# A four-layer graph network on one core: 0/1 matrices made by GpSimd in layer 0's late units, list loads placed later, and the sums of layer 2's nodes split around the edge products

## The reference, cut to what matters

```python
x = _layernorm(x + L0(x, src, dst))             # attention by edges, sums by target node
x = _layernorm(x + L1(x, edge_index))           # sum of neighbours, two-layer network
x = _layernorm(x + L2(x, edge_index))           # graph attention with self loops
x = _layernorm(x + L3(x, edge_index, edge_attr_256))
# inside L0
score = exp(clip(sum(k[src] * q[dst], axis=-1) / sqrt(32), -5, 5))
wv = segment_sum(v[src] * score, dst); z = segment_sum(score, dst)
out = wv / (z + 1e-09)
# inside L2, per head: e = leaky_relu(a_src[src] + a_dst[dst]), softmax over the edges of a
# target, out = segment_sum(h[src] * alpha, dst) + bias, then + x and a layer norm
```

## Time and profile before

| | us |
|---|---|
| median of 3 executions (4677.53 to 4684.41) | 4681.47 |
| the profiled execution, own time | 4724.27 |
| its span in the trace | 4722.6 |

### The profile page before, as it was taken

How to read it: one execution, slowest core, us unless ns; L and a number is a source line. 1 busy time by engine, 2 the same in 40 slices (tenths; PEclk the granted TensorE clock), 3 DMA queues, 4 the chain that set the end, 5 groups by cost and what they waited for, 6 DMA issues and landing times. The chain is left out here.

```text
span 4722.6 us, 90136 instructions
## 1 busy us (share of the span) xinstructions
PE 4413.9 (93%) x21114; PEld 3442.3 (73%) x21114; DVE 3984.7 (84%) x12084; ACT 2635.3 (56%) x6042; POOL 3105.5 (66%) x3736
## 2 busy tenths in 40 slices
PE   6999998769999999999987999999969999999998
PEld 4666664438888888888866777777746666688887
DVE  4677778988999999999974888988867777888887
ACT  2787886544555555555553777777741111255554
POOL 4555552227777777777746888888746666588887
PEclk8999997559999999999997999999989999999999
DMA  5977777983444444444445899999855555788885
GB/s 156 244 219 223 222 219 247 296 251 106 153 152 152 148 149 152 152 152 147 150 155 161 274 275 274 277 274 274 259 158 175 175 175 175 228 260 261 263 261 173
DMA packets 911651, 970.50 MB, mean 206 GB/s; under 512 B 104938, under 2 KB 867672, under 8 KB 911306
## 3 DMA queue, kind: packets, MB, share of 16 engines
q1 hardware_dynamic: 501268, 472.10, 34.2%
q10 hardware_dynamic: 327254, 315.21, 19.6%
q0 software_dynamic: 82784, 179.41, 13.2%
HBM read 654.95 MB, written 363.57 MB: 216 GB/s over the span
## 5 line engine op out<-in xcount | busy, mean ns | idle before, releaser
L601 POOL DMA_INDIRECT layer_xg<-in_x,edge_rows x392 | 387.2, 988 | 332.7 <-PE layer_t_ps L647 240.8
L936 POOL DMA_INDIRECT nodes_near_rows<-x_d,nodes_cur x392 | 418.1, 1067 | 238.1 <-POOL nodes_cur L931 169.8
L1669 POOL DMA_INDIRECT layer_xg<-x_d,edge_rows x392 | 377.6, 963 | 211.3 <-PE layer_x_ps L1742 139.5
L1244 POOL DMA_INDIRECT nodes_near_rows<-hh_d,source_row x392 | 396.0, 1010 | 128.2 <-issue 84.7
L1059 PE MATMUL nodes_h_ps<-w_h,nodes_x2T 128*128 128x272 f32 x1568 | 392.2, 393 | 8.1 <-ACT nodes_x2T L1136 8.1
L1817 ACT ACTIVATE layer_xT<-layer_x_ps 128x512 f32<-128x512 f32 x196 | 117.0, 597 | 495.5 <-PE layer_x_ps L1742 446.2
L680 PE MATMUL layer_agg<-layer_msg,layer_hot 128*128 128x264 f32 x784 | 313.1, 539 | 65.8 <-issue 65.8
L1069 PE MATMUL nodes_hid_ps<-nodes_zT,w_a 128*128 128x256 f32 x1568 | 372.3, 380 | 0.7 <-ACT nodes_zT L1143 0.7
L662 PE MATMUL layer_kv_ps<-w_kv,layer_xT 128*128 128x512 f32 x784 | 371.2, 596 | 0.9 <-DVE layer_made L806 0.9
L1049 PE MATMUL nodes_out_ps<-w_b,nodes_hid 128*128 128x256 f32 x1568 | 371.1, 380 | 0.6 <-ACT nodes_hid L1128 0.5
L1757 PE MATMUL layer_kv_ps<-w_kv,layer_xT 128*128 128x512 f32 x784 | 370.4, 595 | 0.0
(11 more groups left out here) (241 smaller groups left out, 12724.1 us busy)
## 6 DMA issues: line engine op xcount, KB each, us to landing
layer_msg<-msg_d SPq DMA_DIRECT2D x784, 132.0 KB, 3.3
nodes_xin<-x_d SPq DMA_DIRECT2D x392, 256.0 KB
hh_d<-nodes_hh ACTq DMA_DIRECT2D x196, 264.0 KB
x_d<-layer_y ACTq DMA_DIRECT2D x196, 256.0 KB
x_d<-nodes_x2b ACTq DMA_DIRECT2D x196, 256.0 KB
nodes_hin<-hh_d SPq DMA_DIRECT2D x196, 256.0 KB
x_d<-nodes_x ACTq DMA_DIRECT2D x196, 256.0 KB
layer_xin<-x_d SPq DMA_DIRECT2D x196, 256.0 KB
```

The lines of the kernel that those rows point to most:

```text
L601: gp.indirect_dma_start(out=xg[:, c % 8, k, :], out_offset=None, in_=x, in_offset=bass.IndirectOffsetOnAxis(ap=edge_rows[:, c, k:k + 1], a ...
L936: gp.indirect_dma_start(out=near_rows[:, r, h, :], out_offset=None, in_=x1_d, in_offset=bass.IndirectOffsetOnAxis(ap=cur[:, r, h:h + 1], a ...
L1244: gp.indirect_dma_start(out=near_rows[:, u % NR, h, :], out_offset=None, in_=hh_d, in_offset=bass.IndirectOffsetOnAxis(ap=source_row[:, 2 ...
L1669: gp.indirect_dma_start(out=xg[:, c % 8, k, :], out_offset=None, in_=x3_d, in_offset=bass.IndirectOffsetOnAxis(ap=edge_rows[:, c, k:k + 1] ...
```

## The change

1. Layer 0, units from LATE = 104 on: GpSimd makes the two 0/1 matrices behind its load of x, and counts them on a new semaphore. The mean is written back into `agg` in PSUM instead of `mean_msg` in SBUF, so that PE waits before refilling `agg` for the add of x (`filled`) and not for the multiply (`divided`). The merged moments go to `t_ps`, the PSUM tile in which chunks were turned. For all units, DVE's eps-add now stands before the inversion of the norm.
2. Layer 0: GpSimd gathers the lists before chunk 7, not before chunk 4.
3. Layer 2's nodes: PE sums tile 0 ahead of the edge products and tile 1 behind them; the transposes of the shares stand between tile 0's sums and the edge products; ACT copies `own_first` before it copies the edge products. The order inside the step is otherwise as before, and so are the instructions.
4. Layer 3: SP's loads of `e_row` for chunks 2 to 7 wait until PE has turned the chunk two before.

The core of the diff (pieces with nothing but the passing of the new argument are left out):

```diff
+        def late_moments(u):
+            return t_ps[:, u % 4 * 4:u % 4 * 4 + 4].rearrange("p (h w) -> p h w", w=2) if u >= LATE else None
...
-                    if c == 4:
+                    if c == 7:
...
                 for u in range(LATE, UNITS):
                     load_x(gp, u)
+                    gp.wait_ge(summed, u - 3)
+                    for h in range(2):
+                        last = gp.tensor_scalar(hot[:, u % 4, h, :], iota[:, :], target_rel[:, 2 * u + h:2 * u + h + 1], None, ALU.is_equal)
+                    last.then_inc(late_hot, 1)
...
-                            pe.wait_ge(hot_ready, u + 1)
-                            if u >= 2:
+                            if u < LATE:
+                                pe.wait_ge(hot_ready, u + 1)
+                            else:
+                                pe.wait_ge(late_hot, u - LATE + 1)
+                            if u >= LATE + 2:
+                                pe.wait_ge(ln["filled"], u - 1)
+                            elif u >= 2:
                                 pe.wait_ge(divided, u - 1)
...
-                            u = at(U0 + 4)
-                            if u is not None:
-                                norm_invert(ve, ln, (None, 8, u))
                             u = at(U0 + 2)
                             if u is not None:
                                 ve.wait_ge(summed, u + 1)
                                 nc.vector.tensor_scalar(den[:, u % 2, :, :], agg[u % 2][:, :, D:D + H], 1e-9, None, ALU.add)\
                                     .then_inc(eps_added, 1)
+                            u = at(U0 + 4)
+                            if u is not None:
+                                norm_invert(ve, ln, (None, 8, u))
                             u = at(U0)
-                            if u is not None:
+                            if u is not None and u < LATE:
                                 if u >= 4:
                                     ve.wait_ge(summed, u - 3)
                                 one_hot_halves(ve, (None, 8, u), 4, hot, hot_ready)
...
-                                nc.vector.tensor_tensor(by_head(mean_msg[:, u % 2, :, :]), by_head(agg[u % 2][:, :, 0:D]),
+                                to = mean_msg[:, u % 2, :, :] if u < LATE else agg[u % 2][:, :, 0:D]
+                                nc.vector.tensor_tensor(by_head(to), by_head(agg[u % 2][:, :, 0:D]),
                                                         over_head(den[:, u % 2, :, :]), ALU.mult).then_inc(divided, 1)
                         c = chunk_at(s, j)(2)
...
-                                norm_merge(ve, ln, (None, 8, u), spare_ve)
+                                if u == LATE:
+                                    ve.wait_ge(copied, EC)
+                                norm_merge(ve, ln, (None, 8, u), spare_ve, late_moments(u))
...
+                                mean = mean_msg[:, u % 2, :, :] if u < LATE else agg[u % 2][:, :, 0:D]
+                                nc.vector.tensor_tensor(ln["rows"][:, u % 4, :, :], mean, xin[:, u % 8, :, :], ALU.add)\
...
+                def half_of_sums(u, h):
+                    cols = agg[u % 4][:, h * D:(h + 1) * D]
+                    nc.tensor.matmul(cols, hot[:, u % HOT, h, :], weighted[:, u % WR, h, :], start=True, stop=False)
+                    nc.tensor.matmul(cols, ones3[:, :], bias3[:, 0:D], start=False, stop=False)
+                    return nc.tensor.matmul(cols, ident[:, :], own[:, u % WR, h, :], start=False, stop=True)
...
-                        to = agg[u % 4]
...
-                        for h in range(2):
-                            cols = to[:, h * D:(h + 1) * D]
-                            nc.tensor.matmul(cols, hot[:, u % HOT, h, :], weighted[:, u % WR, h, :], start=True, stop=False)
-                            nc.tensor.matmul(cols, ones3[:, :], bias3[:, 0:D], start=False, stop=False)
-                            last = nc.tensor.matmul(cols, ident[:, :], own[:, u % WR, h, :], start=False, stop=True)
-                        last.then_inc(filled, 1)
+                        half_of_sums(u, 0)
+                    g = at(15)
+                    if g is not None and g % GU == 0:
+                        g //= GU
+                        n = of_group(g) * H
+                        pe.wait_ge(share_ready, g + 1)
+                        if g:
+                            pe.wait_ge(weighed, GU * g)
+                            pe.wait_ge(own_done, GU * g)
+                        nc.tensor.transpose(share_ps[:, 0:n], share[0:n, 0, :], ident[0:n, 0:n])
+                        nc.tensor.transpose(own_ps[:, P:P + n], share[0:n, 1, :], ident[0:n, 0:n]).then_inc(share_turned, 1)
...
-                    g = at(15)
-                    if g is not None and g % GU == 0:
...
-                        nc.tensor.transpose(own_ps[:, P:P + n], share[0:n, 1, :], ident[0:n, 0:n]).then_inc(share_turned, 1)
+                    u = at(18)
+                    if u is not None:
+                        half_of_sums(u, 1).then_inc(filled, 1)
                     u = at(15)
...
+                        own_product(u)
...
+                    g = at(15)
+                    if g is not None and g % GU == 0:
+                        g //= GU
+                        n = of_group(g) * H
+                        act.wait_ge(share_turned, g + 1)
+                        if g >= 2:
+                            act.wait_ge(own_summed, GU * (g - 1))
+                        nc.scalar.activation(own_first[:, g % 2, 0:n], own_ps[:, P:P + n], ACT.Copy, scale=-1.0 / BIG).then_inc(first_copied, 1)
                     u, e, k = at(2), at(2 + LATER), s - 2
...
                     if had(c, 8):
                         sp.wait_ge(joined, num(c) - 7)
+                    elif had(c, 2):
+                        sp.wait_ge(turned, num(c) - 1)
                     sp.dma_start(e_row[:, ring(c, 8), :], e_rows[:, bass.ds(num(c), 1), :].rearrange("p c w -> p (c w)"))\
                       .then_inc(e_in[ring(c, 8)], 16)
```

56 lines of the change are left out of this document (22 added, 34 removed).

## The result

The changed kernel takes 4631.92 us in the median of 4 executions (4627.67 to 4633.51), the kernel before 4681.59 (4677.53 to 4684.41): a ratio of 0.9893, 95% interval 0.9876 to 0.9910, so 49.7 us less (42 to 58). The forecast was 4633.

A forecast was written before the change was run, and what follows sets the result against it. Limits were taken by stage: DVE in layer 0's unit-only phase, near PE's limit in layer 2's nodes, first loads at starts. Gains 29 + 11 + 5 + 3 = 48 off the median 4681.5 gave 4633 us, range 4606 to 4668.

The forecast's parts named there:

- The sum (29): Layer 0's late units: 92 steps take 2.37 us instead of 2.69, gaining 29 us (bounds 24 and 31).
- PE's loop at 2.32: Layer 0's late units: PE's wait to refill `agg` allows 2.32 us a step at worst, just under DVE's 2.37.
- Rival (a): Layer 0's late units: DMA tops out near 300 GB/s, step 2.65 us, total gain 23, 4659 us; chance 0.13.
- Rival (d): Layer 0's late units: GpSimd's matrices block DVE for 1.22 us a step, 83 us lost, 4746; chance 0.04.
- Rival (e): Layer 0's late steps stay at 2.6 to 2.7 us, layer 2's own_first stays norm-bound: 4670 to 4680; chance 0.07.
- 13 for `own_first`: Layer 2's turn steps, one in 8: ACT's copy `own_first` starts 0.53 us earlier, gaining 13 us over 24.5 steps.
- 2 lost to the smaller cover: Layer 2's near-scores steps: PE stands 0.1 us for the late turned copy, losing 2 us over 24.5 steps.
- The chain: Layer 2's regular steps: own product through DVE and ACT to `e_row` takes 5.12 us, holding steps at 4.38, no gain.
- rival (b): Layer 2's nodes: the chain doesn't hold, PE's 4.12 us binds, 171 regular steps gain 44 more, 4589; chance 0.04.
- (c): Layer 2's nodes: edge products wait for ACT's turned copy every step; at 0.65 us, 64 lost, 4697; chance 0.04.
- The clock: Layer 2's nodes: shortening the 1.58 us wait removes most falls of PE's granted clock, gaining 5 us (0 to 11).
- The starts: Layer 0's later list gathers taken as 0 (bounds +5 and -5), layer 3's delayed `e_row` loads as 3 (0 to 9).

## Why the prediction was right, and where not

The late units. The sum (29) and the measured 28.8 in the trace and 27 in the median agree, and so do its parts: 2.372 us a step against 2.37. The wait behind the eps-add and the inversion in it were read right; their swap alone is 5.7 of the 29 us. PE's loop at 2.32 was not the bound, and PE didn't stay at half clock either. Rival (a) fell: 336 GB/s were there. (The 350 of the earlier trace rows that spoke against it are of a stretch of 10 us, which is four units and not ten; and in the page's table the slice with PE at 7, DVE at 9 and the clock at 5 is the eighth, not the ninth.) Rival (d) fell too, with an add of 0.67 us; its break-even was miscounted, since 48 us over 92 units are 0.52 us, 0.43 of a pair of 1.22 and not 0.65. Rival (e) fell: no step is at 2.6, and `own_first` came earlier. But the row of L1020 was read too simply: it showed that such a pair blocks one side, and with the mean in SBUF it was the other side that waited.

Layer 2's regular groups. 13 for `own_first` was 0.56 a group (13.7), 2 lost to the smaller cover was 0.11 a group (2.7): 11 in all, measured 0.45 x 24 = 10.8. The 2 came out by luck: the stall it was made of isn't there, and as much is lost one step on. Where PE idles in the turn step was read wrongly (0.5 for `turned`; it is 0.70 for DVE's L1427, ahead of the transposes), and the run with the transposes behind the edge products shows that this wait costs nothing. The chain was read rightly (5.12, and 5.11 after), so rival (b) fell, and so did (c): PE waited for the turned copy once in 800 us, for 0.2. The count of steps in (b) is too high: beside the turn step the one with the near scores isn't regular either (5.09 us before), so there are 147 regular steps, not 171, and 38 us in place of 44. Opening the chain earlier then gave 35 us.

The clock. This term was mis-sized: 5 against 10. I had priced a fall as 0.7 us by a window of 3.4 us with a mean of 0.79. That window lies 2 us too late; the same length from 2802.30 us on is all at half clock (1.2 instead of 2.4 GHz), with PE busy throughout:

```profile
2802.30:2805.70 3.40, 3.40 (x10) 2.59 (x10) 2.67 (x11) 2.24 (x5) 2.13 (x2) 0.50 0.56 196
```

By the same formula a fall is 3.4 x 0.5 = 1.7 us of work, and its step does take 5.78 us instead of 4.10. The group gets a little back: 39.53 instead of 38.13, so one costs 1.40. Seven such groups stand in the steady part of the stage, 9.8 us. That the long wait brings the fall was read rightly as far as the runs show: with its 1.58 us cut to 1.0, or in two, the falls go. Why only one group in three fell is open.

The starts. 3 was forecast; nothing of it is in layer 3, and in layer 0, where I took 0, no gain is shown. So 48 was 29 + 11 + 5 + 3, and the measured 50 is 28.8 + 10.8 + 10. The two main terms are right; that the total came within 2 us is luck in so far as two misses, 5 too little for the clock and 3 too much for the starts, cancel.

The base. The profiled execution lay 43 us over the median, and the terms were taken off the median as absolute numbers. That held, since those us lie at the starts of stages, of which no term was made but the 3; a profiled run near 4676, as forecast, would have needed the same slow starts, and it came at 4633.51.

## What to carry to other kernels

When a step is set by a chain over several engines, find the instruction that opens it and move that, rather than filling the time around it: here 0.97 us earlier for one small matmul was worth more (33 us) than all of the stage's edits in the change (21 us), and the split of the sums paid only once that was done. Put an independent instruction between a producer and its reader on the same engine: 0.06 us a step, 5.7 us in all. Before pricing a fall of the clock by a window, move the window until its mean is lowest, or compare a step with the fall to one without. Compare starts unit by unit before believing a difference of two traces; two traces of one kernel differed by 38 us, nearly all at the starts of stages.

## What the runs showed of the hardware

- The same kernel took 4683 us in one block and 4727 and 4729 in two others, each on a chip of its own. Between two traces of it, 4722.6 and 4684.2 us long, the difference lies at the starts of three stages (13.6, 12.3 and 13.5 us); the steady parts agree to 1 us in 900.
- DVE's add of two SBUF operands beside GpSimd's comparisons, also in SBUF, kept its 0.68 us, while GpSimd's pair went from 1.20 to 1.63. With one operand of the add in PSUM, comparisons beside it took hardly longer than others (0.62 and 0.60 us each).
- PE's granted clock fell to half for 3.4 us behind a single wait of 1.58 us in seven of some 22 steady groups, at 1.40 us for such a group. With one wait of 1.0 us a group it did so once (38.97 us, near the stage's end), and with 0.70 and 0.18 us, as in the changed kernel, in none of the steady groups.
